# New places in the hand-over order for every operation of a four-layer gated cross-attention network

## What is computed

```python
x = x + tanh(g_xattn[l]) * attention_l(x, ctx)
x = x + tanh(g_ffn[l])   * ffn_l(x)
# attention 0: 16 heads of 64; 1 and 3: 16 heads of 8; 2: one head of 128
# ffn 0: gated, weights ternary, activations quantized; ffn 1: 8 experts, top 2 of 8, bounded capacity
# ffn 2: ternary fc -> gelu -> layer norm -> ternary projection; ffn 3: ternary, relu squared, RMS norm
```

## Time and profile before

| quantity | value |
|---|---|
| median of 3 runs | 460.28 us (460.01 to 460.66) |
| the profiled execution | 458.76 us |
| its span, first to last instruction | 456.9 us |
| outside the span | 1.86 us |
| mean granted TensorE clock in the span | 0.914 |
| busy in the span: PE, DVE, ACT, POOL | 382.5, 282.6, 261.8, 181.4 us |
| chain that ended last, by engine | PE 54%, DVE 13%, POOL 9%, ACT 9%, issue 8%, DMA 6% |

### The profile page before, as it was taken

One profiled execution on the slowest core, in us unless ns is written; L12 is line 12 of the kernel. 1 busy time (PEld: TensorE's weight loads), 2 busy tenths in 40 slices (PEclk: granted clock), 3 DMA queues, 4 the chain that ended last, 5 costly groups with the idle time before them and its releaser, 6 DMA issues.

```text
span 456.9 us, 10018 instructions
## 1 busy us (share of the span) xinstructions
PE 382.5 (84%) x3564; PEld 277.6 (61%) x3564; DVE 282.6 (62%) x859; ACT 261.8 (57%) x781; POOL 181.4 (40%) x294
## 2 busy tenths in 40 slices
PE   3789999999999999999952999616778999999943
PEld 1557877777776655655641899504546677766621
DVE  2263586677786897654661221184466478999994
ACT  3148567677677787687631534044384767556542
POOL 4594444232443512142773000288674442331220
PEclk9599999999999999999995899955599999999975
DMA  8991000000000030000003132110000000000001
GB/s 336 393 382 71 2 1 3 1 0 2 2 1 1 9 132 3 2 6 9 30 30 101 36 118 76 41 35 23 23 2 0 2 3 2 1 2 2 4 0 47
DMA packets 7136, 22.12 MB, mean 48 GB/s; under 512 B 1215, under 2 KB 3503, under 8 KB 6575
## 3 DMA queue, kind: packets, MB, share of 16 engines
q1 hardware_dynamic: 6063, 19.38, 11.8%
q0 software_dynamic: 1024, 2.10, 1.6%
HBM read 14.60 MB, written 6.88 MB: 47 GB/s over the span
## 4 chain that ended last, share of the span: by engine, by line
PE 54%; DVE 13%; POOL 9%; ACT 9%; issue 8%; DMA 6%; SPq 1%; POOLq 0%; DVEq 0%; ACTq 0%
PE bank L783 7%; ACT prob L498 5%; PE bank L984 5%; PE bank L810 4%; PE bank L852 4%; PE bank L975 4%; DMA mask_i<-mask_d 4%; PE bank L766 3%; PE bank L832 2%; PE bank L861 2%; PE bank L754 2%; PE bank L820 2%; DVE mx L1209 2%; PE bank L798 2%; PE bank L928 2%
## 5 line engine op out<-in xcount | busy, mean ns | idle before, releaser
L498 ACT ACTIVATE prob<-bank,mx 128x128 f32<-128x128 f32 x256 | 81.8, 384 | 25.9 <-DVE mx L1209 21.8
L1209 DVE TENSOR_REDUCE mx<-bank 128x4 f32<-128x512 f32 x96 | 64.0, 681 | 35.9 <-PE bank L783 24.1
L418 POOL TENSOR_TENSOR prob<-prob,rden 128x512 f32<-128x512 f32 x32 | 33.4, 1044 | 60.7 <-DVE rden L1231 60.6
L391 POOL TENSOR_SCALAR rstd<-mv 128x1 f32<-128x1 f32 x64 | 12.7, 198 | 79.3 <-DVE mv L1184 76.0
L393 POOL TENSOR_TENSOR rstd<-rstd,minus_half 128x1 f32<-128x1 f32 x72 | 41.5, 576 | 6.0
L483 ACT ACTIVATE probT<-bank 128x512 f32<-128x512 f32 x64 | 39.3, 626 | 3.8 <-PE bank L810 3.8
L810 PE MATMUL bank<-pack,prob 128*128 128x128 f32 x256 | 39.6, 279 | 1.4 <-ACT prob L498 0.8
L438 POOL DMA_INDIRECT moe_rows<-yrows_d,row_of x16 | 15.7, 984 | 52.2 <-DMA yrows_d<-o_n 48.2
L810 PEld LDWEIGHTS bank<-pack,prob 128*128 128x128 f32 x256 | 28.6, 141 | 10.8 <-issue 6.1
L783 PE MATMUL bank<-kz,qz 64*128 64x512 f32 x96 | 26.8, 633 | 1.9 <-ACT qz L483 1.2
L498 ACT ACTIVATION_READ_ACCUMULATOR prob<-bank,mx 128x1 f32 x128 | 28.3, 221 | 0.0
(11 more groups left out here) (234 smaller groups left out, 966.9 us busy)
## 6 DMA issues: line engine op xcount, KB each, us to landing
yrows_d<-moe_rows SPq DMA_DIRECT2D x2, 1510.0 KB, 21.3
pack<-pack_d SPq DMA_DIRECT2D x1, 2112.0 KB, 15.7
expert<-experts_d SPq DMA_DIRECT2D x4, 514.0 KB, 8.7
pack<-experts_d SPq DMA_DIRECT2D x4, 514.0 KB, 4.9
pack<-pack_d SPq DMA_DIRECT2D x1, 2048.0 KB, 10.3
xrows_d<-moe_rows SPq DMA_DIRECT2D x1, 1080.0 KB, 21.0
moe_rows<-xrows_d SPq DMA_DIRECT2D x8, 135.0 KB, 3.2
yrows_d<-o_n SPq DMA_DIRECT2D x8, 135.0 KB, 1.8
```

Source lines behind the costliest of these rows:

```text
L418: pool.tensor_tensor(part, part, r.to_broadcast([P, GH, P]), ALU.mult).then_inc(E[A0]["norm"].sem, 1)
L498: act.activation(prob[:, g % 2, P * j:P * j + P], bank[S_BANK[g % 2]][:, P * j:P * j + P], ACT.Exp, bias=mx[:, g % 2, j:j + 1], **kw).then ...
L1209: dve.tensor_reduce(out, bank[S_BANK[g % 2]][:, :].rearrange("p (h t) -> p h t", h=GH), AX.X, ALU.max, negate=True).then_inc(E[layer]["max ...
```

## The change

Every operation gets a new place, on all four engines; nothing else is different. The same operations with the same instructions, waits and buffers are emitted, in another order. The new places come from a planner whose model of the kernel now counts each of GpSimd's operations with the time of its hand-over to the next engine. The diff replaces the numbers of all tables. What follows is its core: POOL's table without F0 to ROUTE, and of the other engines the lines on which the prediction rests.

```diff
@@ -451,30 +451,30 @@
-    (rs, A0, (-25.083, 23.918, 32.313, 57.517, 62.269, 77.402, 78.694, 125.511)),
-    (norm0, 0, (39.107, 52.228, 67.182, 78.694, 99.539, 114.064, 130.676, 142.956)),
-    (norm0, 1, (47.805, 63.052, 74.093, 81.531, 108.314, 115.639, 132.351, 154.79)),
-    (fetch_ahead, (299.517, 308.016, 308.348, 326.972, 333.074, 340.178, 306.785, 316.672)),
-    (rs, A2, (306.189, 307.024, 309.756, 327.68, 331.982, 337.185, 341.372, 343.062))],
-    walk(stages, [(26.8, masks), (295.1, first_fetches)])
+    (rs, A0, (-14.883, -5.182, 40.213, 55.317, 70.669, 88.002, 99.794, 119.211)),
+    (norm0, 0, (37.207, 52.628, 58.482, 79.294, 94.439, 108.964, 125.476, 149.156)),
+    (norm0, 1, (43.805, 55.752, 70.093, 79.931, 104.914, 118.639, 130.051, 149.29)),
+    (fetch_ahead, (295.817, 318.916, 316.948, 327.072, 331.574, 341.178, 314.385, 311.972)),
+    (rs, A2, (305.089, 306.024, 324.056, 327.88, 329.082, 334.685, 343.472, 349.862))],
+    walk(stages, [(11.6, masks), (288.3, first_fetches)])
...
@@ -623,65 +623,65 @@
-    (gelu_e, (268.412, 272.235, 277.805, 282.513, 291.121, 300.93, 303.54, 309.282))],
-    (xt_sb, A2, (309.599, 311.837, 317.759, 332.765, 334.765, 342.47, 348.581, 351.745)),
-    (exps2, (314.158, 317.613, 331.897, 335.604, 339.204, 348.953, 350.61, 356.092)),
-    (probsT_sb2, (329.45, 330.175, 332.884, 336.484, 340.946, 349.122, 355.364, 359.891)),
-    (ot_sb, A2, (331.565, 336.172, 337.872, 343.372, 346.164, 352.907, 361.834, 362.799))],
-    (gelu2, (346.07, 352.235, 356.162, 365.834, 372.954, 384.637, 390.93, 402.868)),
-    (xq_sb, F3, (406.998, 420.587, 429.423, 438.799, 450.752, 457.585, 462.126, 469.525)),
-    (sumsq3, (417.578, 426.565, 436.14, 446.869, 457.544, 461.073, 467.644, 475.879)),
-    walk(stages, [(267.8, route_exp), (311.3, lambda: k4_sb(1, 0))])
+    (gelu_e, (273.212, 273.335, 289.505, 294.713, 295.221, 299.53, 301.74, 303.982))],
+    (xt_sb, A2, (306.199, 311.337, 317.859, 330.265, 331.065, 341.57, 349.481, 353.045)),
+    (exps2, (307.858, 325.613, 328.597, 337.504, 339.204, 346.653, 351.01, 354.092)),
+    (probsT_sb2, (313.75, 326.675, 331.184, 338.384, 345.446, 348.822, 352.664, 357.191)),
+    (ot_sb, A2, (319.165, 335.872, 339.572, 347.172, 348.864, 353.907, 360.634, 362.399))],
+    (gelu2, (345.87, 352.335, 355.162, 361.134, 371.554, 385.737, 395.93, 401.768)),
+    (xq_sb, F3, (415.098, 418.287, 427.523, 440.499, 452.352, 458.385, 472.426, 484.225)),
+    (sumsq3, (417.578, 424.065, 437.64, 449.569, 460.944, 470.573, 482.944, 490.879)),
+    walk(stages, [(283.8, route_exp), (313.1, lambda: k4_sb(1, 0))])
...
@@ -1034,87 +1034,87 @@
-    (xt, A2, (310.271, 316.279, 319.241, 323.603, 325.565, 332.127, 339.414, 344.088)),
-    (scores2, (313.619, 319.027, 321.389, 328.551, 329.813, 337.975, 341.062, 344.418)),
-    (probsT2, (320.697, 321.759, 324.021, 331.183, 332.645, 341.332, 345.107, 350.549)),
-    (pv2, (322.094, 322.111, 327.873, 334.235, 335.406, 341.477, 347.78, 351.945)),
-    (ot2, (322.538, 327.9, 331.962, 335.024, 339.405, 344.995, 353.46, 354.114)),
-    (y, A2, (323.048, 329.51, 333.872, 336.742, 341.098, 351.367, 358.532, 363.654))],
-    (xt, F3, (403.649, 412.323, 424.948, 437.039, 449.091, 455.288, 464.965, 470.48)),
+    (xt, A2, (312.471, 315.979, 316.741, 322.503, 323.765, 333.927, 341.014, 344.988)),
+    (scores2, (313.819, 317.427, 319.089, 323.851, 329.113, 337.975, 342.262, 345.118)),
+    (probsT2, (315.097, 319.659, 324.221, 333.583, 337.545, 339.832, 343.607, 347.949)),
+    (pv2, (318.294, 322.511, 329.873, 336.935, 338.306, 341.177, 345.78, 351.645)),
+    (ot2, (319.438, 328.1, 332.962, 339.824, 339.905, 345.595, 351.76, 352.114)),
+    (y, A2, (320.648, 331.61, 334.372, 340.942, 344.898, 348.367, 357.132, 364.054))],
+    (xt, F3, (402.549, 413.623, 424.148, 438.139, 446.491, 458.188, 471.965, 475.68)),
...
@@ -1520,71 +1520,71 @@
-    (sum_stats, (313.89, 315.435, 317.902, 322.235, 323.875, 332.618, 340.317, 345.37)),
-    (top2, (322.995, 326.728, 329.754, 333.162, 339.262, 344.962, 348.259, 352.373)),
-    (norm2, (327.254, 330.295, 334.501, 340.101, 344.254, 349.804, 354.742, 360.469)),
-    (resid, A2, (338.061, 339.462, 340.365, 341.916, 346.826, 358.651, 364.075, 370.67))],
-    (scale3, (402.079, 412.292, 420.579, 431.854, 440.985, 446.372, 461.447, 466.518)),
-    (square3, (417.994, 423.58, 436.454, 444.384, 450.66, 460.591, 463.058, 486.293)),
-    (hq3, (420.48, 427.568, 437.856, 445.984, 454.49, 461.621, 466.989, 488.923)),
-    walk(stages, [(62.9, means), (273.6, weigh_experts), (316.8, start_last), (416.2, squared_bias)])
+    (sum_stats, (312.39, 312.835, 315.002, 318.735, 324.075, 329.518, 340.917, 344.07)),
+    (top2, (314.595, 319.928, 331.854, 336.862, 337.062, 343.162, 351.359, 354.973)),
+    (norm2, (319.554, 334.295, 336.101, 340.901, 343.454, 344.504, 355.442, 359.969)),
+    (resid, A2, (332.661, 337.662, 341.865, 350.116, 355.326, 359.551, 362.375, 369.67))],
+    (scale3, (403.779, 411.892, 418.379, 431.454, 441.385, 447.472, 462.447, 467.318)),
+    (square3, (413.394, 427.48, 432.354, 443.784, 453.46, 459.291, 467.758, 476.793)),
+    (hq3, (418.08, 428.368, 437.856, 447.484, 455.19, 462.721, 475.789, 497.023)),
+    walk(stages, [(68.3, means), (282.4, weigh_experts), (318.2, start_last), (394.4, squared_bias)])
...
```

More of the change, by code:

```diff
@@ L643, in _ @@
+                    (tanh_gate, (93.347, 103.702, 125.345, 140.558, 157.667, 168.355, 181.948, 193.481)),
+                    (hq_sb, F0, (101.954, 122.474, 136.787, 155.493, 168.039, 175.496, 190.831, 201.581))],
                 A1: [
[L644 to L646 removed]
@@ L655, in _ @@
+                    (probsT_sb, A1, 1, (168.593, 182.184, 195.017, 203.386, 211.04, 226.094, 238.449, 254.244)),
+                    (exps, A1, 3, (170.721, 183.512, 196.545, 203.413, 211.767, 226.521, 239.776, 259.752)),
+                    (probsT_sb, A1, 2, (172.449, 188.399, 197.19, 204.045, 216.397, 228.45, 241.207, 262.18)),
+                    (probsT_sb, A1, 3, (173.499, 189.935, 198.779, 205.632, 222.186, 231.94, 244.146, 266.604))],
                 ROUTE: [
-                    (xt_sb, ROUTE, (197.645, 208.62, 216.974, 233.927, 244.304, 252.175, 259.259, 266.992))],
+                    (xt_sb, ROUTE, (201.645, 210.22, 214.374, 234.327, 249.704, 258.675, 268.159, 269.092))],
@@ L1075, in _ @@
                 ROUTE: [
-                    (xt, ROUTE, (190.317, 199.811, 212.415, 227.719, 237.123, 248.148, 257.372, 261.24)),
-                    (logits, (195.46, 206.763, 217.567, 229.871, 237.764, 248.336, 259.325, 261.6)),
-                    (places, (197.827, 211.93, 221.334, 235.338, 240.863, 250.872, 260.035, 262.442))],
+                    (xt, ROUTE, (189.417, 202.311, 210.815, 224.119, 236.723, 247.848, 253.872, 261.24)),
+                    (logits, (193.56, 208.463, 220.567, 228.571, 240.364, 250.636, 257.225, 262.8)),
@@ L1084, in _ @@
[L1084 to L1092 removed]
+                    (xt_e, (264.184, 264.849, 269.454, 269.963, 279.435, 281.407, 294.779, 302.051)),
@@ new lines, in _ @@
+                    (hidden, 'h0', (264.469, 269.674, 274.923, 279.095, 281.867, 296.239, 301.111, 304.651)),
+                    (hidden, 'h1', (264.879, 269.684, 275.578, 279.75, 284.522, 297.794, 301.366, 305.406)),
+                    (hidden, 'h2', (266.889, 269.861, 275.633, 279.905, 284.877, 299.249, 302.421, 305.561)),
+                    (hidden, 'h3', (267.399, 274.716, 275.888, 280.26, 291.532, 300.304, 302.676, 307.716)),
+                    (down, (275.852, 276.524, 277.996, 292.368, 300.24, 305.812, 307.952, 308.572))],
@@ L1150, in _ @@
             prepare()
-            walk(stages, [(309.5, start_last)])
+            walk(stages, [(311.9, start_last)])
         @block.vector
@@ L1556, in _ @@
+                    (row_numbers, (207.842, 220.224, 229.579, 239.128, 249.449, 256.075, 261.028, 266.118))],
                 MOE: [
-                    (xeT_sb, (269.641, 274.748, 282.362, 284.261, 287.273, 292.282, 293.39, 294.698)),
-                    (y_sb, (284.522, 284.732, 293.44, 296.448, 300.658, 306.166, 309.609, 311.328))],
+                    (xeT_sb, (269.141, 279.448, 279.662, 291.361, 294.973, 296.282, 297.19, 304.098)),
+                    (y_sb, (285.822, 292.232, 296.94, 300.148, 300.558, 304.966, 307.109, 308.228))],
```

304 lines of the change are left out of this document (146 added, 158 removed).

## The result

The changed kernel took 455.2 us (median of 4 runs, 453.65 to 456.85), the kernel before 460.14 us beside it: a ratio of 0.989, with an interval of 0.9855 to 0.9929. It is faster by 1.1%; the forecast was 461.8 us, slower by 0.3%. Two further sets of runs gave 0.990 (0.987 to 0.994) and 0.989 (0.985 to 0.993). The profiled execution took 455.64 us with a span of 453.8, against 458.76 and 456.9 before. So the profiled pair differs by 3.1 us where the medians differ by 4.9; the rest is that the profile of before lay 1.4 us under its median, and the one of after 0.4 above its own.

What follows compares the result with a forecast made beforehand. PE was taken as full except at the start, the way into A2 and the end, where DVE is full. Terms 0 + 0 + 1.5 + 0 gave 460.3 us profiled, plus 1.5 to the median: 461.8 us, range 456.5 to 465.5.

Steps and rivals of the forecast that it cites:

- Start to ROUTE: Start to 249 us: savings hidden behind PE's full queue, value 0, bounded by 3 us either way.
- a fetch off by more than 1 us: Sign at the first fetch: if it moves by more than 1 us, the zero up to ROUTE is wrong.
- MOE and the tables: 249 to 291 us: two new table loads, 1.28 us each, covered on ACT; cost 0, bounds 0 and 2.8.
- The way into A2: 291 to 350 us: chains between engines decide; PE waits behind probsT2[5], A2's end lags; +1.5 us, bounds 0 and +3.0.
- the +1.5 of the sum: Whole kernel: 0 + 0 + 1.5 + 0 us, all of it the lag at A2's end.
- rival (3): Way into A2: stalls behind probsT2[5] keep the clock low ten more us; +3.5 us, 465.3 us; chance 0.07.
- A3 and F3: 350 us to the end: PE full, then DVE, no idle left to win on PE; value 0, end bounds -1.5 and +0.8.
- `scale3[7]` ahead of `square3[6]`: At the end on DVE: 1.5 us earlier, about 1.4 given back because xq_sb[7] stands behind sumsq3[6]; value 0.
- (1): Faster: PE's 8.0 us idle from 34 to 230 us partly filled, 3 us regained, A2 lag swallowed; 457.3 us; chance 0.32.

Runs made afterwards that it cites:

- re_new: The kernel before with new places up to ROUTE and from A3 on, old ones in MOE, A2 and F2; ratio to before 0.989 (0.986 to 0.993).
- w_new: The kernel before with new places only from the first fetch to where A3 begins (A2, first batches of F2); ratio to before 1.000 (0.997 to 1.002).
- e_new: The kernel before with new places only from A3 on, with the rest of F2; ratio to before 0.996 (0.993 to 0.999).
- after_again: The changed kernel run once more, nothing altered; ratio to before 0.990 (0.987 to 0.994), 456.43 us.
- end_first_part: The kernel before with new places only from the start of A3 up to place 385; A3's first queries to last matmul 103.77 us, before 104.61.
- gpsimd_only: The kernel before with new places up to ROUTE for GpSimd alone; 472.16 us, slower by 2.4% (1.021 to 1.028).
- after_third: The changed kernel run again, nothing altered, on the same chip as a further run; ratio to before 0.989 (0.985 to 0.993), 455.3 us.

## Why the prediction was wrong, step by step

**Start to ROUTE: 0 forecast, -1.5 us measured** (235.1 against 236.6), within the 3 us either way that bounded it. PE stayed as full as it was read; but 8.0 us of idle time were known, and that a new order would leave them as they are was a choice, not a reading. The last scatter was 1.3 us and the first fetch 1.2 us earlier, and a fetch off by more than 1 us was the sign that the prediction had named for this zero being wrong. In MOE 0.2 us of it went back in the profiled pair and 0.6 in `re_new` (45.2 instead of 44.6 us), with the longer stretch at half clock.

**MOE and the tables: right.** 17 loads, and this is what stands between the experts, timeline of ACT in after, to be read beside the earlier trace rows:

```profile
256.27 0.49 ACT L602 ACTIVATE k<-bank,expert 128x270 f32<-128x270 f32 x1 [0.24 <-PE bank L975]
256.77 1.28 ACT L621 ACT_TABLE_LOAD   x1
258.07 0.21 ACT L621 ACTIVATE w_tok<-w_tok 128x16 f32<-128x16 f32 x1
258.30 1.28 ACT L602 ACT_TABLE_LOAD   x1
260.26 1.62 ACT L602 ACTIVATE k<-bank,pack 128x270 f32<-128x270 f32 x4 [0.67 <-PE bank L984]
```

`gelu_e[2]` waits for PE for another 0.67 us after both loads, so they are covered, and PE is busy for 41.94 of 42 us. The Trainium skill ("ScalarE: Activation LUTs", section "What ACT_TABLE_LOAD costs") would have about 2.66 us for each switch; here the instruction behind a load starts 1.30 us after the load does, so the rows' price was the right one.

**The way into A2: the chain was read well, its value was not.** As forecast, `top2[0]`, the load and the exp of batch 0 run early, `start_last` and `k4_sb` late. DVE in after (answers the earlier trace rows):

```profile
303.33 0.29 DVE L1243 TENSOR_REDUCE mx<-bank 128x1 f32<-128x128 f32 x1 [3.09 <-PE bank L905]
...
316.22 0.34 DVE L1191 SCALAR_TENSOR_TENSOR pack<-bank,tanh_g,pack 128x128 f32<-128x128 f32 x1
```

`resid[0]` is at 316.22, 4.2 us nearer to the fetch than before, where 3.3 was forecast, and F2's first `up` at 34.1 us from the fetch instead of 35.75, where 0.4 later was forecast. Then PE waits for `probsT2[5]`, 2.25 us for the 2 forecast. `xt[6]` comes at 331.97, 39.5 us after the fetch where it was 38.2: 1.3 later, and not the 3.0 forecast. In the profiled pair the stretch is 1.3 us longer, close to the +1.5 of the sum, but by luck: `up` was 2.1 us better than forecast, and the 1.5 us that were to be made up behind `xt[6]` were not. The runs of `w_new` give 0.0%, and the likely reason is the clock, rival (3), whose two sides the prediction didn't see. Windows of 6 us of before (column 1.00 or 0.50 near the end is the clock):

```profile
324.00:330.00 6.00, 4.87 (x19) 3.72 (x18) 2.90 (x13) 2.74 (x9) 3.82 (x7) 0.50 0.09 22
330.00:336.00 6.00, 4.05 (x21) 2.30 (x19) 3.94 (x17) 4.26 (x13) 4.30 (x9) 0.97 0.02 4
336.00:342.00 6.00, 4.96 (x31) 3.38 (x30) 3.85 (x14) 5.73 (x10) 4.98 (x11) 1.00 0.00 0
```

of after:

```profile
330.00:336.00 6.00, 4.59 (x16) 2.61 (x17) 3.26 (x14) 3.75 (x11) 3.35 (x8) 0.72 0.02 4
336.00:342.00 6.00, 5.19 (x30) 4.41 (x28) 2.67 (x9) 3.94 (x10) 2.99 (x6) 0.71 0.00 0
```

and of `e_new`, whose order in A2 is that of before, instruction for instruction:

```profile
330.00:336.00 6.00, 4.93 (x17) 2.87 (x15) 3.05 (x12) 3.43 (x9) 3.65 (x9) 0.50 0.02 4
336.00:342.00 6.00, 5.42 (x26) 3.96 (x26) 2.77 (x10) 4.74 (x10) 4.49 (x9) 0.69 0.00 0
```

In before the clock was full from 330.4 us; in `e_new` only from 339.7; in after it came at 329, fell after the wait, at 332.6, and came back at 339.5. Counted from the first fetch, the same old order takes 54.4 to 55.1 us to A3 where the clock returns after 33 to 38 us (seven traces, in two of them with a fall of 3 us behind that), and 56.4 to 56.9 where it returns after 46 to 47 (four). The new one took 55.9, 56.7 and 55.9 where the clock came after 37 us, fell behind the wait and came back after 47, and 56.3 (`after_again`) where it came only after 47.3. The new order thus costs 1 to 2 us against the early course and gains some 0.5 us against the late one (a single trace). Rival (3) put the price of a low clock at 3.5 us; between its two courses the old order differs by 2. How many of the runs of before and of `w_new` took which course can't be read from their times, so that the clock accounts for the 0.0% is argued and not shown. The profiled execution of before had the early one; the prediction saw that it lay 1.5 us under the median, and carried that along as a constant instead of asking which stretch it came from.

**A3 and F3: 0 forecast, -2.65 to -3.3 us measured.** This is the step that failed, and the largest term. It read PE's 1.1 us of idle time in the earlier trace rows as "no idle is left to win" and put the stretch at 0. `e_new` shows 2.65 us won there with the old order everywhere else. New places up to place 385 give 0.8 us and those behind it 2.0, and of these 2.0 us 1.3 are busy time of PE, not idle time: that PE is busy was no floor. The last batches have 0.8 us of the gain, see below. DVE, the full engine behind 395 us (33.45 of 35 us), idled for 13.5 us from 350 to 395, in the same row. In the 20 us from A3's first queries, the window of before:

```profile
348.27:368.27 20.00, 18.59 (x188) 12.91 (x189) 10.47 (x29) 11.90 (x22) 7.87 (x16) 1.00 0.01 2
```

and of `e_new`:

```profile
350.08:370.08 20.00, 19.24 (x194) 13.54 (x196) 12.20 (x33) 12.48 (x24) 8.08 (x18) 1.00 0.01 2
```

DVE does 12.2 instead of 10.5 us of its work. (Between 350 and 395 us, as the expectation had it, `e_new` has only 0.6 us less idle time, since its A3 began 1.8 us later.) Its waits in those windows, for scores (L783) and for a hidden layer's `rs` (L1355), before:

```profile
DVE mx L1209 <- PE bank L783: 5.4, 3, 3.4
...
DVE hid L1355 <- POOL rstd L393: 0.9, 1, 0.9
```

In `e_new` the first row is 4.7 and the second is gone. That work done early spares DVE time later is plausible, but `end_first_part`, with the same 12.2 us, won only 0.8 us: it bounds this part, and what wins the rest between place 385 and the last scores stays open. At the end, `scale3[7]` ahead of `square3[6]` did what was forecast for it, with the sizes off: from A3's last output projection on PE (L895) to `xt[7]` it is 6.4 us where it was 7.6 (6.5 in `e_new`), so 1.2 won (forecast 1.5), and from `xt[7]` to the last matmul 8.5 instead of 8.1, so 0.4 given back (forecast 1.4, on the strength of `xq_sb[7]` behind `sumsq3[6]`).

**The rivals.** (1) was the one that came: the 8.0 us of idle time were partly filled, by 1.6 us, though not by `norm0` alone, as `gpsimd_only` shows. It was priced at 457.3 us: it took 3 us from the start, where 1.5 came, and lacked the end. That this lies near the 455.2 measured is luck in part. The range ended at 456.5, too high by 1.3: it took 3 us either way "once" for the whole kernel and allowed the end 1.5 us, where the two together gave more. The chance of a faster kernel, 0.32, was too low: with 8 us of PE idle and 13.5 of DVE idle open to a new order, both signs should have been even at least.

## What to carry to other kernels

Don't put a stretch at 0 because its engine is full: here a stretch with 1.1 us of idle time on PE in 45, followed by one that is full on DVE, gave 2.65 us. Ask also which engine bounds what follows; idle time of that engine is a chance, though here at most 0.8 us of 1.7 filled was won by it. Read a change of order as one unit; a single engine's new order, tried alone, can cost 2.4% where all together save 1.1%. Before one profile is compared with another, ask which course the clock took in each, stretch by stretch. And when an operation is waited for, look at what stands ahead of it on its own engine (a gelu and its table load) before moving the one that waits.

## What the runs showed of the hardware

The clock of a stretch is not a property of the kernel alone. It came and went at moments that differed by up to 9 us between executions of the same order (full again at 330.4 us in before and 339.7 in `e_new`, in A2), it fell for 3 us near 31 us in 8 of the 18 traces of this case, with the old table there and with the new, and one such fall costs 0.9 to 1.7 us. The record of the clock is not complete: in after it lacks the half clock at the start, which the 2.08 us of the first eight k matmuls give away against 1.16 in `after_third`. Runs of one kernel spread over 457.3 to 463.1 us (27 runs of before on one chip). The Trainium skill ("TensorE: Matmul & The Clock Gate", Part 1) has the clock follow what PE did recently; the falls behind PE's waits agree with that. Why executions of one order got different courses, no run here shows.
